# Layer 0's expert sum: two of four experts on VectorE, two on TensorE

## What is computed

```python
scores = jax.nn.softmax(logits, axis=-1)
topk_w, topk_i = jax.lax.top_k(scores, K_TOP)          # K_TOP = 4
...
down = jnp.einsum('bsek,ekh->bseh', activated, down_proj) + down_bias
sel = jnp.take_along_axis(down, topk_i[..., None], axis=2)
out = jnp.sum(sel * topk_w[..., None], axis=2)
...
h = h + _L0_ffn_ref(_layernorm(h, axis=-1), ...)
h = h + _L1_attn_ref(_layernorm(h, axis=-1), ...)
```

## Time and profile before

| | |
|---|---|
| median of three runs | 751.5 us (750.11, 756.46, 751.5) |
| span of the profiled execution | 760.1 us |
| TensorE busy | 683.2 us, 90% |
| VectorE busy | 419.2 us, 55% |
| GpSimd busy | 267.3 us, 35% |
| ScalarE busy | 244.9 us, 32% |
| mean granted TensorE clock | 0.980 |
| TensorE's filler products (L284) | 155.7 us busy, 1210 entries |

### The profile page before, as it was taken

The page is one execution under the profiler, slowest core; times in us unless marked ns, Lnnn a source line. Parts: engine busy times, 40 slices in busy tenths (PEclk is TensorE's granted clock), DMA queues, the critical chain, the costliest instruction groups (busy, mean ns, idle before and its releaser), DMA issues. The chain is left out here.

```text
span 760.1 us, 19172 instructions
## 1 busy us (share of the span) xinstructions
PE 683.2 (90%) x7307; PEld 516.5 (68%) x7307; DVE 419.2 (55%) x1088; ACT 244.9 (32%) x577; POOL 267.3 (35%) x308
## 2 busy tenths in 40 slices
PE   7998789899888889989998898999998899889996
PEld 5776679744333768854476786786435678889996
DVE  4846657776665264767634755656792565612211
ACT  1034321145555033134512511434463162111110
POOL 2427532335553230144323434701462312243220
PEclk9999899999999999999999999999999999989999
DMA  9502239744443439565522256201563133937403
GB/s 354 245 1 50 21 117 389 265 120 133 140 141 102 149 85 409 204 207 179 169 92 50 22 206 230 22 5 37 169 221 113 54 35 119 366 102 283 157 26 106
DMA packets 77120, 112.03 MB, mean 147 GB/s; under 512 B 44070, under 2 KB 57575, under 8 KB 74087
## 3 DMA queue, kind: packets, MB, share of 16 engines
q1 hardware_dynamic: 66469, 88.26, 35.2%
q0 software_dynamic: 6144, 15.21, 6.5%
q10 hardware_dynamic: 4418, 7.33, 2.6%
HBM read 96.68 MB, written 14.11 MB: 146 GB/s over the span
## 5 line engine op out<-in xcount | busy, mean ns | idle before, releaser
L284 PE MATMUL ps<-const_sb 128*128 128x128 f32 x1210 | 155.7, 284 | 10.2 <-DMA const_sb<-in_consts 4.7
L284 PEld LDWEIGHTS ps<-const_sb 128*128 128x128 f32 x1210 | 146.8, 198 | 17.5 <-issue 12.1
L2073 PE MATMUL ps<-l_w,const_sb 128*32 (+1 forms) x236 | 98.0, 545 | 13.4 <-ACT const_sb L2161 9.0
L2073 PEld LDWEIGHTS ps<-l_w,const_sb 128*32 128x32 f32 (+1 forms) x236 | 26.8, 121 | 58.0 <-issue 54.3
L1064 PE MATMUL ps<-x_fm,w_sb 128*128 128x296 f32 x208 | 54.9, 415 | 4.8 <-PEq L241 4.4
L2115 PE MATMUL ps<-l_w,row_sb 128*32 (+1 forms) x214 | 55.7, 387 | 0.6 <-ACT row_sb L2189 0.6
L312 POOL TENSOR_TENSOR norm_r<-norm_ve,const_sb 128x2 f32<-128x2 f32 (+1 forms) x27 | 19.6, 725 | 92.4 <-DVE norm_ve L305 67.1
L1064 PEld LDWEIGHTS ps<-x_fm,w_sb 128*128 128x128 f32 x208 | 38.9, 190 | 18.2 <-issue 6.2
L2073 PE MATMUL ps<-w_sb,const_sb 128*64 128x512 f32 x104 | 49.2, 595 | 0.0
L420 ACT ACTIVATE x_fm<-ps 128x256 f32<-128x256 f32 x35 | 12.3, 383 | 106.8 <-PE ps L393 106.7
L1981 POOL DMA_INDIRECT l0e_y_scratch<-row_sb,l0e_rows_u x26 | 26.6, 1024 | 43.3 <-ACT row_sb L2208 41.4
(11 more groups left out here) (549 smaller groups left out, 1518.3 us busy)
## 6 DMA issues: line engine op xcount, KB each, us to landing
l_w<-in_l_experts SPq DMA_DIRECT2D x1, 8704.0 KB, 26.8
l_w<-in_l_experts SPq DMA_DIRECT2D x1, 8192.0 KB
expert_w<-in_l_experts SPq DMA_DIRECT2D x4, 2048.0 KB
l_more_w<-in_l_experts SPq DMA_DIRECT2D x4, 2048.0 KB
l1e_own_gu<-in_l_experts SPq DMA_DIRECT2D x11, 704.0 KB
w_sb<-in_l_biases SPq DMA_DIRECT2D x52, 128.0 KB
l_w<-in_l_experts SPq DMA_DIRECT2D x1, 6144.0 KB, 20.6
l2e_own_gu<-in_l_experts SPq DMA_DIRECT2D x11, 512.0 KB
```

What stands on the lines that cost most here:

```text
L284: pe.matmul(ps[:, bank, 0:P], ident, ident, start=True, stop=True)
L2073: mm = pe.matmul(to[c * R:(c + 1) * R, :], xg_fm[:, r % 2, k, c * R:(c + 1) * R], own_gu[:, c - 1, r % 2, c0:c0 + wide] if c else whole(wh ...
```

## The change

TensorE's part of the sum begins at expert 2 instead of 1, so `summed` has 10 pairs instead of 15 and ten diagonals are built, in slices 0 to 9. VectorE's `ready` now adds experts 0 and 1: it waits for all transfers of the group, adds expert 0 of each tile, waits for these to end, adds expert 1 of each tile, and waits again. Two other values follow `slots`: TensorE waits for 10 signals of `s_diag` instead of 15, and its first product of a tile is that of expert 2. Line numbers below the edit grow by two, so L2463 and L2470 are L2465 and L2472 in the changed kernel.

```diff
-                slots = range(1, top) if many else range(top)
+                slots = range(2, top) if many else range(top)
...
                         def ready(dve, g):
                             if many:
                                 for t in range(*GROUPS[g]):
-                                    x = h[0:real[t], t, :]
                                     dve.wait_ge(s_back[t], 16)
-                                    signal(dve.scalar_tensor_tensor(out=x, in0=back[0:real[t], 0, t, :],
-                                                                    scalar=share[0:real[t], 0, t:t + 1], in1=x,
-                                                                    op0=ALU.mult, op1=ALU.add))
-                                wait()
+                                for i in range(slots[0]):
+                                    for t in range(*GROUPS[g]):
+                                        x = h[0:real[t], t, :]
+                                        signal(dve.scalar_tensor_tensor(out=x, in0=back[0:real[t], i, t, :],
+                                                                        scalar=share[0:real[t], i, t:t + 1], in1=x,
+                                                                        op0=ALU.mult, op1=ALU.add))
+                                    wait()
                             dve.wait_ge(s_sum, g + 1)
```

## The result

| | before | after |
|---|---|---|
| median | 751.67 us (22 runs, 748.2 to 756.46) | 756.22 us (22 runs, 752.15 to 759.49) |
| ratio to before, 95% interval | | 1.0048 (1.0031 to 1.0064) |
| span of the profiled execution | 760.1 us | 752.9 us |
| mean granted TensorE clock, that execution | 0.980 | 0.977 |
| mean granted clock over the timed runs | 0.9827 | 0.9776 |

The changed kernel is slower by half a per cent, 3.6 us by the ratio. That is inside the stated range and inside the band of 1%, but the interval excludes the forecast of no change. The two clocks in the last row are means over the 22 runs of after and over 28 runs of before that were made beside the first experiments. A few executions on record are far longer than the rest (986.71 us, for example), and the ratios and clocks leave these slow ones out.

A forecast was written before the change was run, and what follows sets the result against it. The stage's end was taken as what TensorE reaches, once VectorE gives it normalized tiles. Terms of -0.71, +0.61, +0.51 and -0.38 gave +0.03 us, so 751.5 us was forecast (760.1 for the profiled execution), range 748.5 to 757.0 us.

The forecast's parts named there:

- (a): Layer 0's expert loop: five diagonal builds leave VectorE, 1.4 us beside TensorE's work, so 0 us gained.
- (b): Layer 0's sum on TensorE: 15 products become 10, saving 2.2 us if nothing else holds.
- (c): Layer 0's sum on VectorE: five more multiply-adds cost 2.33 us of its time, a little more than TensorE saves.
- +0.03 with bounds of 0.4: End of layer 0's sum stage: -0.71 + 0.61 + 0.51 - 0.38 = +0.03 us, bounds -0.4 and +0.4 us.
- Rival 2: TensorE's clock falls in layer 0's sum after longer idling: likelier 1 to 2 us slower, at most 6.7; chance 0.06.

The follow-up runs named there:

- the first experiments: Four kernels on one chip: after with 15 diagonals 1.0058; before without expert 1's products 1.0050, with VectorE's second pass added 1.0016, with ten diagonals 0.9999.
- the second profile of before: Profile of the unchanged kernel before, run again as a kernel of its own for control; timed at 1.0003 against before.
- the profiles at -20: Eight profiles of kernels with 20 entries less than before in TensorE's stream; kernels timed at 1.0048, 1.0058, 1.0050, 1.0029 and 1.0052.
- those at 0: Six profiles of kernels with as many TensorE stream entries as before; kernels timed at 1.0016, 0.9999, 1.0023, 0.9986 and 1.0003.
- the second series: After timed once more against before, on the chip that also timed after with one two-column product per tile: 1.0052, beside 0.9986 for the latter.
- the ten tiny products: Before with ten products of 2 columns added ahead of the 28 fillers of layer 0's sum, 40 stream entries more: 0.9976.

## Why the prediction was wrong outside the stage, and right inside it

**(a) Builds, 0 us.** Right: 0.9999 with five builds less, and the loop takes 84.95 us from the first L2249 to the last with 15 builds (the second profile of before) and with ten. The pairs quoted from the earlier trace rows, 2.82 and 2.83 us apart, were slices that caught up behind a disturbed one. The conclusion held, its evidence was poor.

**(b) TensorE saves 2.2 us of its own time, none of it at the end.** Right. It ended group 0's products early and waited 1.19 us ahead of tile 2 (over 1 us was forecast).

**(c) VectorE.** From TensorE's first product, L2472 of group 0 came at +2.39 us (forecast +2.2), that of group 1 at +6.26 (+6.0), the turn of tile 2 at +11.53 (+11.2). Each is 0.2 to 0.3 us late. The start was mis-sized: the multiply-adds began 0.56 us behind TensorE's first product (250.75), where 0.40 us had been taken (258.84 - 258.44). Four of them then took 1.79 us (1.78). In group 1 they started 0.18 us behind L305, 0.10 us later than the sum had it. The stage cost +0.36 us where +0.03 with bounds of 0.4 had been worked out: a miss within its bounds. What was not said is that TensorE would wait 1.17 us for the first normalizing.

**Rival 2** had a true mechanism at the wrong place. In the sum the clock fell in one of five profiles of after and just so without the change, for 2.3 us; at the end of the program it fell in all five, but in the first profile of before too. The price of 1 to 2 us was near.

**The step that failed** is the sentence "Layer 1 starts behind a barrier of all engines, so this difference is carried on whole". It takes all that follows as unchanged because its work is. The work was, and its place in TensorE's stream was not. Leaving out 20 entries, with no other edit, costs 0.5% and 0.3% in two series (1.0050, 1.0029); 20 entries without work, put back, take the whole edit's loss away (0.9986 beside 1.0052). In the layer 2 stretch it is 1.6 us between the means (115.53 - 113.91), at the end of the program 1.1 us (16.17 - 15.07). With the sum's 0.36 us that is 3.1 of the 3.6 us. That the time stayed inside the stated range is no merit of the sum: the range was set by the scatter of the kernel's own runs.

**What stays open** is whether these parts are the whole. They were picked where the kernels differ. From layer 1's first product to the end the profiles at -20 take 483.6 us on average (480.6 to 485.6) and those at 0 482.4 us (479.4 to 484.9), 1.3 us more and not 3.6, since the stretches between give a part back. Single executions are too few for more. Part of the loss goes with the clock: over the runs the mean granted clock is 0.9776 at after and 0.9825 at before. A core that is at half speed for a share x has a mean of 1 - x/2, so that is 2 x 0.0051 x 752 = 7.7 us more at the lower level. Within the 22 runs of after the time rises by 0.49 us for each 0.001 of mean clock lost, which makes 2.5 us of the difference. This overlaps with the parts above, since three of the eight layer 2 stretches and all eight ends hold such falls. In the second series the clocks are closer (0.9802 and 0.9824, 1.1 us by that slope) at the same loss, so the clock is not all of it either. And the edit's own cost at an equal place lies between -0.1% and +0.3% by the kernels that have it (0.9986, 1.0023, 1.0006 against 0.9976), and no run narrows it. The two with the edit and a longer stream have the short end of the program (12.93 and 13.02 us), yet were timed at 1.0008 and 1.0006; why they don't gain what before gains is not known.

**A version that beats both** is before with ten fillers more (0.9967 and 0.9973, about 2.3 us). By the ten tiny products (0.9976) its gain is mostly of place: 2.0 us at the end of the program (15.07 - 13.04) and 1.7 us in layer 2's stretch (113.91 - 112.26), of which other stretches take a part back. The next edit of TensorE's stream may take the rest.

## What to carry to other kernels

On an engine with thousands of short instructions, an edit also moves everything behind it in the instruction stream. Before a difference of half a per cent is ascribed to the edit, run a control that pads the stream to its old length with instructions that do almost nothing, and compare where the pauses marked "issue" and the block transfers of the instruction queue fall. Sum an edit's cost in its stage, but give the rest of the program a term of its own, here between -0.3% and +0.5%. And take a span from one profile as one execution: the first one here held 8 us that no other had.

## What the runs showed of the hardware

- TensorE's pauses marked "issue" in layer 2's attentions are pinned to the number of the instruction, whole multiples of 256 records apart. They end 1.19 to 1.61 us behind the end of a 16 KB transfer of queue 8 and are up to 1.89 us long.
- At the program's end the last scatter's return was issued 2.35 us behind the scatter's start where no block transfer began beside it, and 3.51 to 4.21 us behind it where one began 1.38 to 2.13 us in. The longer wait went with a fall of the clock, 6.24 us in place of 4.56 us for the last sum.
- 20 stream entries more or less moved the whole kernel by up to 0.5%, at nearly equal work. 60 entries less did not do more than 20 less (1.0020).
- The granted clock fell to 0.58 over 4 us of the sum in some executions of kernels with and without the change, and cost 2.3 us in the one profile of after that has it.
- In one execution four slices of the expert loop waited for a releaser outside the program's engines, 11.9 us in sum for VectorE, of which the loop lost about 8 us.
